# Layer 1 attention: the adapter scores of a later unit issued between the weighing and the transposed adapter product

## The reference

```python
q, k, v = split_heads(hidden @ Wq), split_heads(hidden @ Wk), split_heads(hidden @ Wv)   # 32 heads of 8
q, k = rope(q), rope(k)
w = softmax(q @ k.T / sqrt(8) + mask)                      # self attention
attn = w @ v
a_k, a_v = split_heads(adapter @ Wk), split_heads(adapter @ Wv)   # adapter = ctx_2048
a_w = tanh(gate) * softmax(q @ a_k.T / sqrt(8))            # adapter attention
attn = attn + a_w @ a_v
x = x + tanh(g_xattn[1]) * (attn @ Wo)
```

## Time and profile before

| what | value |
|---|---|
| median of three runs | 1927.67 us |
| lowest, highest | 1916.81, 1933.82 us |
| the profiled execution's own time | 1921.5 us |
| its span, first to last instruction | 1920.2 us |
| TensorE / VectorE / ScalarE / GpSimd busy, share of the span | 88% / 70% / 49% / 41% |
| mean granted TensorE clock | 0.956 of full speed |
| layer 1 attention, from its first adapter keys to its last output projection | 576.4 to 938.6 us of the span |

### The profile page before, as it was taken

The page is one execution under the profiler, slowest core; times in us unless marked ns, Lnnn a source line. Parts: engine busy times, 40 slices in busy tenths (PEclk is TensorE's granted clock), DMA queues, the critical chain, the costliest instruction groups (busy, mean ns, idle before and its releaser), DMA issues.

```text
span 1920.2 us, 35897 instructions
## 1 busy us (share of the span) xinstructions
PE 1696.0 (88%) x12175; PEld 1177.6 (61%) x12205; DVE 1336.7 (70%) x4259; ACT 947.2 (49%) x2211; POOL 791.6 (41%) x957
## 2 busy tenths in 40 slices
PE   6989898979988999999796877778999999988998
PEld 2444444647756777777674554556777777766445
DVE  7888873624467888889647898864667667666447
ACT  2776674214424777777554555324444444443352
POOL 3333321176746656664625553220243333443350
PEclk7999999999997999999997999799999999999998
DMA  4454421139854443333214542028010000030857
GB/s 112 99 130 102 102 55 49 55 130 354 304 140 88 94 89 81 80 84 68 86 38 112 161 109 78 11 67 297 1 37 19 33 11 2 14 99 25 260 194 309
DMA packets 179669, 200.41 MB, mean 104 GB/s; under 512 B 85732, under 2 KB 149361, under 8 KB 176160
## 3 DMA queue, kind: packets, MB, share of 16 engines
q1 hardware_dynamic: 163456, 156.31, 29.9%
q0 software_dynamic: 15168, 41.54, 6.1%
q10 hardware_dynamic: 864, 0.26, 0.1%
HBM read 131.88 MB, written 75.44 MB: 108 GB/s over the span
## 4 chain that ended last, share of the span: by engine, by line
PE 53%; DVE 23%; ACT 8%; POOL 6%; issue 6%; DMA 2%; SPq 0%; DVEq 0%; ACTq 0%; POOLq 0%
PE psum L3400 3%; PE psum L3474 3%; DVE sbuf L539 3%; PE psum L389 3%; PE psum L1337 2%; PE psum L352 2%; PE psum L3449 2%; PE psum L1058 2%; PE psum L1702 2%; PE psum L3467 2%; PE psum L1356 2%; ACT sbuf L3837 2%; PE psum L2286 2%; PE psum L3436 2%; PE psum L1767 1%
## 5 line engine op out<-in xcount | busy, mean ns | idle before, releaser
L539 DVE TENSOR_REDUCE sbuf<-psum 128x2 f32<-128x512 f32 x256 | 164.4, 683 | 35.0 <-PE psum L352 34.0
L190 POOL TENSOR_TENSOR sbuf<-sbuf 128x1 f32<-128x1 f32 x128 | 73.4, 575 | 273.0 <-DVE sbuf L182 272.7
L2023 ACT ACTIVATE sbuf<-psum 128x512 f32<-128x512 f32 x256 | 137.4, 588 | 45.2 <-PE psum L1767 44.0
L3837 ACT ACTIVATE sbuf<-psum,sbuf 128x128 f32<-128x128 f32 x256 | 113.7, 455 | 88.8 <-DVE sbuf L3649 88.7
L678 ACT ACTIVATE sbuf<-psum 128x1024 f32<-128x1024 f32 x128 | 131.2, 1026 | 47.3 <-PE psum L374 43.0
L3929 POOL DMA_INDIRECT l_slot_inputs<-sbuf x96 | 97.1, 1011 | 100.0 <-DVE sbuf L3720 75.0
L3474 PE MATMUL psum<-sbuf 128*128 128x256 f32 x512 | 123.7, 385 | 4.9 <-DVE sbuf L3667 4.9
L352 PE MATMUL psum<-sbuf 112*128 112x256 bf16 x512 | 104.3, 288 | 15.8 <-DVE sbuf L539 11.1
L3400 PE MATMUL psum<-sbuf 128*128 128x256 f32 x512 | 115.8, 379 | 0.8 <-ACT sbuf L3801 0.8
L1892 DVE CUSTOM_DVE_ANT_0 sbuf<-psum,sbuf 128x128 f32<-128x128 f32 x512 | 112.5, 284 | 1.0 <-PE psum L1746 1.0
L3400 PEld LDWEIGHTS psum<-sbuf 128*128 128x128 f32 x512 | 96.1, 190 | 20.3 <-issue 8.6
(11 more groups left out here) (434 smaller groups left out, 4480.1 us busy)
## 6 DMA issues: line engine op xcount, KB each, us to landing
l_pair_outputs<-sbuf SPq DMA_DIRECT2D x24, 512.0 KB, 6.7
sbuf<-in_l_gu_pairs SPq DMA_DIRECT2D x32, 384.0 KB, 7.1
sbuf<-l_pair_outputs SPq DMA_DIRECT2D x16, 768.0 KB, 14.5
l_q_parts<-sbuf SPq DMA_DIRECT2D x32, 192.0 KB, 2.6
sbuf<-l_q_parts SPq DMA_DIRECT2D x16, 384.0 KB
sbuf<-l_q_parts SPq DMA_DIRECT2D x32, 192.0 KB
sbuf<-l_k_parts SPq DMA_DIRECT2D x32, 192.0 KB
sbuf<-in_l_down_pairs SPq DMA_DIRECT2D x32, 192.0 KB, 8.9
```

The source lines that it names most:

```text
L539: dve.tensor_reduce(top3[:, 2 * hp:2 * hp + 2, c], score_bank[v % 2].rearrange("p (j t) -> p j t", j=2), AXX, ALU.max, negate=True).then_i ...
L2023: act.activation(e_t[i % 4][:, h * BANK:(h + 1) * BANK], turn_bank[:, h * BANK:(h + 1) * BANK], ACT.Exp).then_inc(*exped.up())
L3837: last = act.activation(e_t[u % 3][:, j * P:(j + 1) * P], score_bank[:, j * P:(j + 1) * P], ACT.Exp, bias=mt[:, j:j + 1], scale=rq[:, lo + ...
```

## The change

In each turn `pe_adapter_scores(u + AHEAD + 1)` is issued after `pe_weigh(u - 1)` and ahead of `pe_adapter_turned(u)` and of `pe_pro_slot(2u)`; before it came after both. No instruction is added or taken away, and no wait is changed.

```diff
@@ -1818,11 +1818,11 @@
                 pe_turn(u)
             if 1 <= u <= NS:
                 pe_weigh(u - 1)
+            if 0 <= u + AHEAD + 1 < NS:
+                pe_adapter_scores(u + AHEAD + 1)
             if 0 <= u < NS:
                 pe_adapter_turned(u)
             pe_pro_slot(2 * u)
-            if 0 <= u + AHEAD + 1 < NS:
-                pe_adapter_scores(u + AHEAD + 1)
             if 0 <= u + 3 < NS:
                 pe_scores(u + 3)
             pe_pro_slot(2 * u + 1)
```

## The result

Over 19 timed runs of each, the changed kernel took 1939.02 us in the median (1932.02 to 1944.76 us) and the kernel before 1927.17 us (1916.81 to 1933.82 us). The ratio is 1.0061, with a 95% interval of 1.0049 to 1.0073: slower by 0.6%, 11.9 us, and within 1%. The predicted time was 1928.6 us in a range of 1918 to 1940 us. The forecast "no change beyond 1%" and the direction hold, but the size does not: twelve microseconds, not one, and nearly all of the range was used. Of the rivals, "the falls stay" (1933.4 us) and half of "the transfers take over" (1938.7 us) came nearer than the forecast.

The account below looks back on a forecast made before the run. The stage was taken as close to TensorE-bound, in a loop of waits starting with its own projections. Terms +0.6 + 2.8 + 1.4 + 0.9 - 4.8 = +0.9 us, put on the median of 1927.67, gave 1928.6 us; range 1918 to 1940 us.

Parts of the forecast that it names:

- no change beyond 1%: Whole kernel: the measured time would lie within 1% of the kernel before, chance 0.94.
- the direction: Whole kernel: slightly slower, by +0.9 us.
- the falls stay: Rival, at the five stalls of turns 12 to 44: half-clock falls remain, clock term zero; +5.7 us, 1933.4 us; chance 0.25.
- the transfers take over: Rival, turns 2, 10, ..., 50: scores wait longest for the stacks' loads; +19.0 us, 1946.7 us, at half price 1938.7; chance 0.12.
- The loop through the projections: Turns 0 to 48: later L1702 adds +8.1 us, the group leaving the chain at L1778 saves 7.5 us; sum +0.6 us.
- the clock: Stalls of turns 12 to 44: shorter idle removes four of five half-clock falls, -4.8 us.
- Turn 54: L1778 and the output projection L1800 run behind the scores' transfer wait instead of ahead of it: +1.4 us.
- The wait on the transfers: Turns 2, 10, 18 and 34: moved scores wait 0.7 us each for stack loads, with work queued behind: +2.8 us.
- The wait on the maximum: Turns 3, 11, 19, ...: L1758 waits 0.3 us for VectorE's maximum, hidden by the next stall: zero, at most 1.8 us.
- The start: Turn -1: the values run behind scores that wait for the maximum, 1.3 us later, 0.45 us of it recovered: +0.9 us.
- the gain rival: Thirteen long waits ahead of L1778 filled, all five falls gone: -13.9 us, 1913.8 us; chance 0.16 in part or whole.

Follow-up runs that it names:

- 1: Kernel before, with the adapter scores ahead of L1778 and the projection slot only in turns 0, 2, 5 modulo 8, up to 48; ratio 1.0052.
- 9: Kernel before, with the adapter scores behind L1778 but ahead of the projection slot in turns 0, 2, 5 modulo 8, up to 48; ratio 1.0050.
- 10: Kernel before, with adapter scores and self scores between L1778 and the projection slot in turns 0, 2, 5 modulo 8, up to 48; ratio 1.0087.
- the second: Kernel before, with the adapter scores ahead of L1778 and the projection slot only in turns 4 and 7 modulo 8, below 48; ratio 0.9996.
- The eleventh experiment: Kernel before, with the new order only in turn 54; ratio 1.0038 to the kernel before.
- the sixth experiment: Kernel before, with adapter scores, self scores and slot 2u ahead of L1778 in turns 4 modulo 8, adapter scores alone in 7 modulo 8; ratio 0.9986.
- the twelfth experiment: The sixth experiment, with the adapter scores of unit 60 moved from turn 54 to turn 55 behind the weighing; ratio 0.9965 to the kernel before.
- the seventh experiment: The twelfth experiment, with slot 2u also ahead of L1778 in turns 0, 2, 5 modulo 8, up to 48; ratio 0.9973 to the kernel before.

## Why the prediction came out where it did

**The loop through the projections is right.** The late L1702 costs 0.45 us each, three times in eight turns, and the group leaves the chain twice: shown by 1, 9 and 10 for the first and by the turns 7 modulo 8 of the second for the other. In the changed kernel L1778 of turn 28 starts 25.9 us after turn 24 instead of 25.0 us, that is the two L1702, and the transposes of turn 29 follow it after 2.24 instead of 3.02 us, that is the group at half clock. Over the whole of turns 24 to 31 the two parts leave 0.1 us (three times 0.45, less 0.78 and 0.46 us), and 0.43 us were measured; the other 0.3 us are in turn 29, into which the half clock reaches further. So the mechanism stands, and its sum of +0.6 us is right only to about a third of a microsecond per eight turns.

**The step that failed is the clock:** "I take four of five as gone, -4.8 us". In the changed kernel one of the five was gone (turn 44, with a wait of 2.20 us) and a new one came in turn 4, behind 2.13 us, so five falls stayed five. That is the rival "the falls stay". Nor was the stall shortened as the term has it: it is 2.25 and 2.20 us in turns 28 and 44, but 2.78, 2.74 and 2.77 us in turns 12, 20 and 36, and why it hardly shrank there is open. I had ordered the waits by length alone. The eleventh experiment has turn 4 as before, with the same wait of 2.21 us that kept its clock in the earlier trace rows, and there it fell:

```profile
639.21 1.01 PE L1778 MATMUL psum<-sbuf 128*128 128x128 bf16 x8 [2.21 <-ACT sbuf L2023]
...
640.86 1.06 PE L1758 MATMUL psum<-sbuf 96*128 96x128 bf16 x8
```

So in this range the length of the wait alone does not decide. What else does, no run here separates; where in time the wait falls is my reading. The Trainium skill (TensorE: Matmul & The Clock Gate, Part 1: The HAM clock gate (the "warmup" mystery)) says that the window of the monitor which sets the clock runs freely and does not start anew with the kernel. The two equal waits with different outcomes agree with it, though no run here shows the monitor itself. A term of zero would have fitted.

**Turn 54 was mis-sized:** +1.4 us predicted, +4.1 us in the trace. The two groups behind the transfer were right. Left out were the half clock behind the longer wait, 2.0 us on the groups from L1758 to L1746, and a landing 0.6 us later in the turn.

**The wait on the transfers** was put at +2.8 us in four turns. The trace has waits of 0.86 us in turn 18 and 0.69 us in turn 34 and none in turns 2 and 10. The two turns got 0.93 and 0.75 us longer, so the term was 1.7 us.

**The wait on the maximum** was put at zero in one turn of eight. It stood in 17 places, 7.4 us, two of them at the start and fifteen (4.8 us) later, each but two 0.25 or 0.34 us. In the chain of the first experiment the maximum (L1900, 760.02) stands behind the rotary embedding (L1862, 759.27), which waits for the late L1702; I take this as the cause here too. I had compared it with the maximum's place before the change. Its cost by itself was not separated. In the first experiment turns 0 to 47 are 7.6 us longer than before, where L1702 alone would make 8.1 us, which leaves little for it there, though that trace also has one clock fall less (four instead of five).

**The start** was +0.9 us; the trace has +2.3 us. The changed order takes 1.4 us more than the unchanged one in the mean over the traces, and the rest is within the 1.3 us by which the unchanged start varies.

**Beyond the stage** I had nothing. The feed-forward part is 3.0 us longer in the change's trace, at a lower clock. That it goes with a lower clock is shown by the windows; what puts the clock there on one course or the other is not settled. The terms without the clock sum to +5.7 us. With 2.7 us more in turn 54 and 3.0 us in the feed-forward part it would be 11.4 us, near the 11.9 us of the medians, but in that sum misses of opposite sign cancel, and the two traces it is taken from lie 16.4 us apart. So it was luck in part that the time fell inside the range: the size was missed by 11 us, and the range was wide. Its lower end is given as half of the gain rival, which would be 7 us below the kernel before, and not the 10 us used.

## What to carry to other kernels

Ahead of filling an idle slot on an engine, follow the chain of waits once around the loop: if the idle slot ends a chain that starts with work on the same engine, then what is moved ahead of that work can cost its full length each time round, as it did here, and filling the slot does not pay that back. A group that may wait for a transfer should not stand ahead of work that is ready: the waits in turns 18 and 34 made their turns longer by about their own length, the one in turn 54 by more. And look at the turns one by one: the same edit lengthens the loop in three turns of eight and shortens it in two. Last, time a part of a kernel in more than one execution before a difference of 1 or 2 us in it is given a cause, since one clock fall is worth as much.

## What the runs showed of the hardware

A wait of 2.21 us ahead of TensorE's products was followed by the full clock in one execution and by half clock in another, at the same instruction. Waits of 2.1 to 3.2 us went either way: 2.13 us lost the clock in the changed kernel, 3.13 us ahead of turn 20's L1778 kept it in the first experiment and 3.12 us in its turn 44 did not:

```profile
735.19 0.80 PE L1778 MATMUL psum<-sbuf 128*128 128x128 bf16 x8 [3.13 <-ACT sbuf L2023]
735.83 0.61 PE L1716 MATMUL psum<-sbuf 128*128 128x128 f32 x4
...
870.00 1.01 PE L1778 MATMUL psum<-sbuf 128*128 128x128 bf16 x8 [3.12 <-ACT sbuf L2023]
```

In the sixth experiment the clock fell behind waits of 1.0 and 1.33 us in turns 36 and 37. The half clock stretches cost about 1.2 to 1.6 us each in this stage: eight turns of the sixth and the twelfth experiment took 42.6 us without one and 44.1 to 44.2 us with one; those of the first and the ninth 44.5 and 45.7 us.

The feed-forward part, whose code is the same in all fourteen kernels, took 72.6 to 74.1 us in seven traces and 75.2 to 77.1 us in the other seven. The two windows above show the longer course at a clock of 0.91 and the shorter one at 0.95.

In the seventh experiment every eight turns from 8 on took 44.29 to 44.38 us, each with one such stretch; the first eight took 40.4 us without one. By the price above, an estimate, the later ones would take 42.7 to 43.1 us without. That the turns and the clock keep in step would be one reading; it was not tested.
